# FFN output tiles computed in pairs in a gated cross-attention and FFN kernel

## The reference, cut to what matters

```python
x = x + tanh(g_xattn[0]) * xattn(layernorm(x), ctx, ctx, Wq, Wk, Wv, Wo, bo)   # 16 heads, causal
x = x + tanh(g_ffn[0]) * ffn(layernorm(x), ...)

def ffn(x):                                       # 256 -> 1024 -> 1024 -> 1024 -> 256
    h = silu((x @ w1.T) * s1) * ((x @ w2.T) * s2)
    h = gelu((h @ h1.T) * h1s)
    h = gelu((h @ h2.T) * h2s)
    return (h @ w3.T) * s3
```

## Time and profile before

| what | value |
|---|---|
| time, median of 3 runs | 1852.26 us (1851.1 to 1852.58) |
| the profiled execution: its own time | 1853.97 us |
| the profiled execution: its span | 1852.2 us |
| PE busy | 1775.5 us, 96% of the span, 15622 matmuls |
| PE weight loads (PEld) busy | 1691.6 us, 91%, 15622 loads |
| DVE, ACT, POOL busy | 63%, 70%, 48% |
| granted TensorE clock, mean | 0.978 |

### The profile page before, as it was taken

One profiled execution on the slowest core, in us unless ns is written; L12 is line 12 of the kernel. 1 busy time (PEld: TensorE's weight loads), 2 busy tenths in 40 slices (PEclk: granted clock), 3 DMA queues, 4 the chain that ended last, 5 costly groups with the idle time before them and its releaser, 6 DMA issues.

```text
span 1852.2 us, 47792 instructions
## 1 busy us (share of the span) xinstructions
PE 1775.5 (96%) x15622; PEld 1691.6 (91%) x15622; DVE 1159.0 (63%) x2675; ACT 1291.6 (70%) x3014; POOL 894.7 (48%) x1132
## 2 busy tenths in 40 slices
PE   2489999999999999999999999999999999999998
PEld 2389999999999999999999999999999999999998
DVE  3857665666665566666566766566766556666652
ACT  2467677777667777667777767777766777766764
POOL 3545444555454455554455544455545445555441
PEclk7589999999999999999999999999999999999999
DMA  7844454444544444445444445444444444444420
GB/s 251 229 99 121 130 138 130 114 108 125 136 125 134 120 112 121 125 125 138 125 117 111 126 127 140 130 114 108 125 136 125 132 120 112 122 125 125 131 52 18
DMA packets 399710, 231.43 MB, mean 125 GB/s; under 512 B 287296, under 2 KB 377664, under 8 KB 398144
## 3 DMA queue, kind: packets, MB, share of 16 engines
q1 hardware_dynamic: 394944, 230.77, 46.6%
q10 hardware_dynamic: 4736, 0.28, 0.2%
HBM read 113.53 MB, written 41.94 MB: 84 GB/s over the span
## 4 chain that ended last, share of the span: by engine, by line
PE 74%; DVE 9%; issue 7%; POOL 5%; ACT 3%; ACTq 1%; DMA 1%; POOLq 0%; SPq 0%; DVEq 0%
PE ffn L948 54%; PE work L885 12%; PE s_bank L922 3%; PE pv L939 3%; DVE probs L591 2%; DVE negmax L599 2%; POOL y L505 2%; ACT probs L772 2%; POOL ha_lo L487 1%; POOL p_parts L453 1%; DVE full L626 1%; ACTq L743 1%; DVE full L619 1%; PE work L1034 1%; ACT full L817 1%
## 5 line engine op out<-in xcount | busy, mean ns | idle before, releaser
L948 PE MATMUL ffn<-hb_hi,W 128*128 128x256 f32 x2048 | 516.2, 292 | 1.8 <-DVE hb_lo L633 1.8
L948 PE MATMUL ffn<-ha_hi,W 128*128 128x256 f32 x2048 | 495.4, 284 | 0.9 <-POOL ha_lo L487 0.9
L948 PE MATMUL ffn<-hb_lo,W 128*128 128x256 f32 x2048 | 490.7, 279 | 0.0
L948 PE MATMUL ffn<-ha_lo,W 128*128 128x256 f32 x2048 | 485.8, 279 | 0.0
L453 POOL CAST p_parts<-probs 128x512 f16<-128x512 f32 x256 | 173.8, 679 | 488.5 <-ACT probs L772 482.1
L948 PEld LDWEIGHTS ffn<-ha_hi,W 128*128 128x128 f32 x2048 | 384.2, 188 | 8.9 <-POOL ha_lo L487 5.1
L948 PEld LDWEIGHTS ffn<-hb_hi,W 128*128 128x128 f32 x2048 | 384.4, 188 | 4.8 <-DVE hb_lo L633 2.4
L948 PEld LDWEIGHTS ffn<-hb_lo,W 128*128 128x128 f32 x2048 | 384.8, 188 | 2.4
L948 PEld LDWEIGHTS ffn<-ha_lo,W 128*128 128x128 f32 x2048 | 384.4, 188 | 0.0
L772 ACT ACTIVATE probs<-probs,exp_bias 128x128 f32<-128x128 f32 x1024 | 317.6, 390 | 51.0 <-DVE exp_bias L601 49.9
L455 POOL TENSOR_TENSOR p_parts<-probs,p_parts 128x512 f16<-128x512 f32 x256 | 305.8, 1194 | 20.4
(11 more groups left out here) (86 smaller groups left out, 3023.9 us busy)
## 6 DMA issues: line engine op xcount, KB each, us to landing
k<-k_saved SPq DMA_DIRECT2D x256, 128.0 KB, 2.9
q<-q_saved SPq DMA_DIRECT2D x256, 128.0 KB, 2.8
k_saved<-k_parts SPq DMA_DIRECT2D x32, 512.0 KB, 2.7
q_saved<-q_parts SPq DMA_DIRECT2D x32, 512.0 KB, 2.7
wnat<-in_ffn_w SPq DMA_DIRECT2D x11, 1024.0 KB, 7.0
xT<-in_x_T SPq DMA_DIRECT2D x32, 256.0 KB, 2.9
cT<-in_ctx_T SPq DMA_DIRECT2D x32, 256.0 KB, 2.8
x_in<-in_x SPq DMA_DIRECT2D x32, 256.0 KB, 2.8
```

The costliest lines, as they stand in the source:

```text
L948: return pe.matmul(dst, w, h, **flags)
```

## The change

`hidden` takes two destinations and two weight positions. For each input tile it makes four matmuls: high part with the first tile's weights, high part with the second's, low part with the first's, low part with the second's. The two destinations are the two halves of one bank, and the whole is one accumulation group: start is set on the very first matmul only, stop on the very last only.

For L1 the two are w1 and w2 of the same step. For L2 and L3 the two are output tiles k - 1 and k; nothing is done at the step with the even k, and both are computed at the step with the odd k. So L3.2 moves behind O.0, Q.0+ and Q.1+ on PE, and L3.4 moves behind To.1. Between the other even and odd steps PE has nothing. The number of matmuls and weight loads stays. DVE, ACT, POOL and SP are unchanged.

```diff
-                def hidden(dst, weight_at, tiles, m, his, los, out_width, before_tile=lambda kt: None):
-
-                    n_mm = 2 * tiles
-                    i = 0
+                def hidden(dsts, weights_at, tiles, his, los, before_tile=lambda kt: None):
+
+                    last = [None, None]
                     for kt in range(tiles):
                         before_tile(kt)
-                        for part in (his, los):
-                            at = weight_at + kt * out_width + m * P
-                            last = mm(dst, W[:, at:at + P], part[:, kt], start=i == 0, stop=i == n_mm - 1)
-                            i += 1
+                        for i, part in enumerate((his, los)):
+                            for half in range(2):
+                                at = weights_at[half] + kt * F
+                                last[half] = mm(dsts[half], W[:, at:at + P], part[:, kt], start=kt == 0 and i == half == 0,
+                                                stop=kt == tiles - 1 and i == half == 1)
                     return last
...
-                            hidden(ffn[use][:, 0:TOK], W1_AT, KE, k, x2T_hi, x2T_lo, F)
-                            hidden(ffn[use][:, TOK:2 * TOK], W2_AT, KE, k, x2T_hi, x2T_lo, F).then_inc(l1_ready, 1)
-                        if kind in ("L2", "L3") and ffn_on:
+                            hidden((ffn[use][:, 0:TOK], ffn[use][:, TOK:2 * TOK]), (W1_AT + k * P, W2_AT + k * P), KE,
+                                   x2T_hi, x2T_lo)[1].then_inc(l1_ready, 1)
+                        if kind in ("L2", "L3") and ffn_on and k % 2 == 1:
...
-                            use, r = ffn_bank(first_use + k // 2), k % 2
-                            if r == 0:
-                                before_ffn(pe, j, first_use + k // 2)
-                            dst = ffn[use][:, r * TOK:(r + 1) * TOK]
-                            if k == 0:
-                                last = hidden(dst, at, KF, k, his, los, out_width, split)
+                            use = ffn_bank(first_use + k // 2)
+                            before_ffn(pe, j, first_use + k // 2)
+                            dsts = ffn[use][:, 0:TOK], ffn[use][:, TOK:2 * TOK]
+                            weights_at = at + (k - 1) * P, at + k * P
+                            if k == 1:
+                                both = hidden(dsts, weights_at, KF, his, los, split)
                             else:
-                                last = hidden(dst, at, KF, k, his, los, out_width)
-                            last.then_inc(ready, 1)
+                                both = hidden(dsts, weights_at, KF, his, los)
+                            for last in both:
+                                last.then_inc(ready, 1)
```

More of the change, by code:

```diff
@@ L984, in body @@
                                 wait(pe, x2lo_ready, ROWS * j + ROWS)
-                            hidden(ffn[use][:, 0:TOK], W1_AT, KE, k, x2T_hi, x2T_lo, F)
-                            hidden(ffn[use][:, TOK:2 * TOK], W2_AT, KE, k, x2T_hi, x2T_lo, F).then_inc(l1_ready, 1)
-                        if kind in ("L2", "L3") and ffn_on:
-                            first_use, at, his, los, out_width, ready, split = {
-                                "L2": (L2_USE, H1_AT, ha_hi, ha_lo, F, l2_ready, tile_split),
-                                "L3": (L3_USE, H2_AT, hb_hi, hb_lo, F, l3_ready, pair_split(l2_lo))}[kind]
-                            use, r = ffn_bank(first_use + k // 2), k % 2
-                            if r == 0:
-                                before_ffn(pe, j, first_use + k // 2)
-                            dst = ffn[use][:, r * TOK:(r + 1) * TOK]
-                            if k == 0:
-                                last = hidden(dst, at, KF, k, his, los, out_width, split)
-                            else:
-                                last = hidden(dst, at, KF, k, his, los, out_width)
-                            last.then_inc(ready, 1)
+                            hidden((ffn[use][:, 0:TOK], ffn[use][:, TOK:2 * TOK]), (W1_AT + k * P, W2_AT + k * P), KE,
+                                   x2T_hi, x2T_lo)[1].then_inc(l1_ready, 1)
@@ new lines, in body @@
+                        if kind in ("L2", "L3") and ffn_on and k % 2 == 1:
+                            first_use, at, his, los, ready, split = {
+                                "L2": (L2_USE, H1_AT, ha_hi, ha_lo, l2_ready, tile_split),
+                                "L3": (L3_USE, H2_AT, hb_hi, hb_lo, l3_ready, pair_split(l2_lo))}[kind]
+                            use = ffn_bank(first_use + k // 2)
[4 more added lines that the diff above has]
+                                both = hidden(dsts, weights_at, KF, his, los, split)
+                            else:
+                                both = hidden(dsts, weights_at, KF, his, los)
+                            for last in both:
+                                last.then_inc(ready, 1)
```

## The result

The changed kernel takes 1900.3 us (median of 4 runs, 1894.8 to 1901.4) against 1852.4 for the kernel before; the ratio is 1.0254, 95% interval 1.0242 to 1.0266. Slower was forecast, at 1905 us. The profiled execution is the fastest of the four (1894.8 us, span 1893.0). The rows here are of the changed kernel unless said otherwise.

The account below looks back on a forecast made before the run. PE, busy 96% of the span, was taken to bound the kernel, paying every gap in full. 0.59 + 1.38 - 0.26 = 1.71 us per body over 31 bodies, 53.0 us, gave 1905 us from a median of 1852.26; range 1886 to 1915.

Parts of the forecast that it names:

- L2.0's wait: At L2.0's last input tile PE waits for POOL's low part; paired, the wait was to go, -0.26 us a body.
- L3.4 behind To.1: L3.4 hides DVE's and POOL's work between PV.7 and To.1; moved behind To.1, all behind is +1.38 us late.
- L3.2 behind O.0: L3.2 hides O.0's wait for ACT's copy of To.0's result; moved, V+ and all behind are +0.59 us late.
- an end of the cost: Lower end: a pace of 0.113 us in a quarter of the FFN's matmuls, 12 us less in all.
- steps stay at 0.118: Sign that the forecast is right: FFN matmuls on PE keep their pace of 0.118 us a step.
- The restart: PE's effective start after a wait, read at Q.1+ as 0.16 us behind the release and applied to O.0 and To.1.
- No cost of alternating weights: FFN matmuls: zero taken for the changed order of weights, with a load per matmul before and after.
- Rival 3: PE's clock falls because it idles 1.4 us in a row once per body: 42 us more, 1947; chance 0.03.
- Changes of type: Upper end: 0.1 us more at each restart and each change of matmul type, 9 us in all, so 1914.

## Why the prediction was right

The two lost covers and L2.0's wait came as forecast, each in its size, and the waits and the chain are those that were named.

- **L3.4 behind To.1.** Forecast +1.38 us a body. Undoing it alone brought the slow-pace body from 56.78 to 55.37, 1.41. The 0.03 is To.1's second step, 0.137 us in place of 0.108, which the sum did not have.
- **L3.2 behind O.0.** Forecast +0.59. With L3.4 undone and L2.0's gain in, the body is +0.35; with both undone -0.22; so 0.57.
- **L2.0's wait.** Forecast -0.26. Measured -0.22 and -0.23. The row was read in a body whose first steps in L2 ran at 0.113: PE came to the last input tile early and stood there longer. In a body at the slow pace the same two steps take 0.225 and 0.227 us (at 333.96 and 334.18 us before), 0.22 over two usual ones; the mean of 29 bodies is 0.24.
- **What the sum lacked.** With that wait gone, long runs at 0.113 us go on through L2. I had taken that pace as an end of the cost and spread it over a quarter of the FFN's matmuls; in the profiled execution 93 of the 320 steps have it in 24 bodies. So the sign "steps stay at 0.118" did not come. And the last body was not in the sum at all. The sum gave the profiled execution 1907.0 us, and it took 1894.8. Of these 12.2 us, 9.8 are the long runs (24 x 0.41), 2.6 the last body and 1.1 the time before the first body with an FFN (100.70 for 101.82); the slow pace's 1.76 for 1.71 gives 1.6 back. The median is only 5 us from 1905, and that much is luck: how many bodies have a long run was not forecast, and it differs from one kernel to the next.
- **The restart.** The 0.16 us read off Q.1+ is two things: PE starts 0.06 us behind DVE's end, and the next step takes 0.10 more. At O.0 it came out the same, 0.05 behind ACT and 0.10. At To.1 PE starts 0.15 behind POOL's recorded end and the next step takes 0.03 more, 0.17 in all; that this is close to 0.16 was not to be known from Q.1+.
- **No cost of alternating weights.** Right: the kernel with the moves alone, where equal weights stand together, is the slower one. By the Trainium skill's page "TensorE: Matmul & The Clock Gate", "Step-by-step: what each phase is for", weights are loaded once and used by several matmuls, so that order should have been the cheaper. It is not borne out here: a weight load is recorded for every matmul in the changed kernel as before, at the same length as where the weights repeated:

```profile
L948 PEld LDWEIGHTS ffn<-ha_hi,W x2048: 186/188/192, 111.4 to 1869.3; 128*128 128x128 f32 x187
...
L948 PEld LDWEIGHTS ffn<-ha_lo,W x2048: 187/188/189, 111.6 to 1869.5; 128*128 128x128 f32 x187
```

- **The clock.** Rival 3 did not come: in the changed kernel it stays at 1.00 in all bodies shown, with PE idle for 1.3 us in a row in each. In six experiments it falls in the last body with attention, and once in the loop, in the one with PV.0 before L1.7 (0.94 from 156.90 to 217.00 us).
- **Changes of type.** I had no charge in the sum for PV's bf16 matmuls directly ahead of fp32 ones, only 0.1 us for each change of type in the upper end. Here O.0's wait hides it; where that wait was taken away it came out at 0.08 us.
- **The range.** It was written as 1886 to 1915, where the ends as added up are 1885 and 1914; nothing hangs on that.

Not tried: what makes a run start at 0.113 rather than at 0.118 us. And the three executions at 1899 to 1901 us have no profile, so that they differ from the one at 1895 by such runs is only argued: 24 x 0.41 = 10 us would separate none from 24.

## What to carry to other kernels

On an engine that never waits, a step may be there as cover. Before moving one, look at what stands behind it: which result it waits for, when that is ready by the other engines' rows, and what is left in between; the difference is paid in full, once per iteration, and other work of the right length in the same place gets it back. Work of the next iteration gives no cover in the last one. Undo the parts of a change one at a time: this one had a gain of 0.6% in it and a loss of 3.2%, both from the same few lines.

## What the runs showed of the hardware that was not expected

- The same stream of 256-column fp32r matmuls, each with its weight load, runs at either 0.1178 or 0.1133 us a step (the bodies at 328.97 and 893.33 us of the changed kernel). In L2 a run at 0.1133, once begun, lasts to the next wait or change of matmul type: 93 steps, 10.5 us, in each of the changed kernel's 24. It does not take a listed wait for the pace to change: in L1 of the kernel before, 15 steps at 0.113 follow a step of 0.120 in the middle of the layer (up to 327.95 us).
- In fp32, the second step behind bf16 matmuls takes 0.30 us instead of 0.216 (V+ behind PV.7).
- Released from a wait, PE starts 0.05 us behind ACT's recorded end (O.0), 0.06 behind DVE's (Q.1+) and 0.15 behind POOL's (To.1), and its next step is longer too: 0.10 us more for fp32 matmuls of 256 columns, 0.03 for the transposes.
